# Second layer's softmax divisors moved to GpSimd ahead of the transposes, its output projection in three single-pass parts, a full-height halo product, and reordered units, in a fused two-layer kernel

## The chip, the cores and the metric

One core of a Trainium2 chip. TensorE (PE) multiplies and transposes, ScalarE (ACT) and VectorE (DVE) read its results out of PSUM, GpSimd (POOL) works on SBUF only, SyncE (SP) starts transfers. The metric is the time of one execution on the device in microseconds (us), lower is better, as the median of the runs.

## The reference, cut to what matters

Eight images of 384 rows (256 image rows, 128 text rows) and 256 columns go through an edge filter and a text embedding, then two transformer layers, the second with a mixture of eight experts:

```
edge = abs(conv3x3(gray, scharr)).sum / 2          # rows 0..255 of h
h = h + attn0(LN(h))        # 16 heads of 16, causal; then gelu MLP 256-1024-256 inside
h = h + ternary_ffn(LN(h))  # relu, 256-1024-256
# second layer's attention, on LN(h):
att = q @ k.T / 8 + slope * rel            # 16 heads of 64, 4 key/value heads, causal
m = max(att);  e = exp(att - m)
att = e / (1 + sum(e))                     # the divisor is one number per row and head
out = (att @ v).transpose(...) @ Wo        # Wo is 1024 x 256
h = h + out
h = h + moe(LN(h))          # router, top 2 of 8 experts, capacity 960
```

## The kernel before

The attention runs as 16 units, one for each image and layer. `unit` exists once for each engine, and each holds a hand-written list of short calls; a unit's list is the order of that engine's queue. A call that doesn't apply to a kind of unit (`Kind`) does nothing. Units 0 to 7 are the first layer (`U_FIRST`, five `U_MID0`, `U_SIX`, `U_SEVEN`), unit 8 (`U_EIGHT`) is the second layer's first, then come six `U_MID1` and `U_LAST`. Other work lies between a unit's heads: a first-layer unit carries the convolution of a coming image, the previous image's first projection, MLP and ternary feed-forward (s2); a second-layer unit carries the next image's queries and keys (s1p) and the previous image's projection, norm and router (s3). Units 9 to 14 hold s1p and s3 alone, unit 8 holds s2 and s1p, unit 15 s3 alone. After the units come an epilogue for the last image, the routing, and the experts.

Within a unit the 16 heads go in pairs. `scores(p)` (L962) makes a pair's products into PSUM banks 0 to 2; `mask_max(n)` (DVE, L2286) adds the bias, writes `probs[:, n % 4]` and the row maxima; `exps(n)` (ACT, L1725) exponentiates in place and leaves the row sums in `rowsum`; `turn(n, half)` (PE, L978) transposes a head's six 128 x 128 blocks into banks 3 and 4; `take_turned(n)` copies bank 3 (ACT, L1733) and bank 4 (DVE, L2429) to `probsT[:, n % 4]`; `mix(c)` (PE, L1013) multiplies a pair by the values into bank 5. There are four buffers of `probs` and of `probsT`, and `mask_max(n)` comes behind `take_turned(n - 4)` in DVE's queue. `exps` takes the six instructions of a head: three activations and three reads of the accumulator.

The divisors of the second layer go a way of their own. `invert(c)` (DVE, L2300 to L2302) adds 1 to a pair's sums and takes reciprocals; `spread(c)` (POOL, L3178) copies them into `rinv`, 128 x 384; `divisors(c)` (PE, L989) transposes that in three steps into bank 6 or 7; `take_divisors(c)` (ACT, L1644) copies it to `rinvT`; `weigh(c)` (DVE, L2308) multiplies bank 5 by `rinvT` into `o1T[:, c, :]` and frees bank 5. `spread`, `divisors` and `take_divisors` of the last pair are done in the next unit (`..._last`). The first layer does the same in two groups of eight heads.

`second_rows(t)` (PE, `token_major`, L1030 with tiles `wo,o1T`) is the second layer's projection: for each of three row tiles eight products 128x128 by 128x256 in fp32. The epilogue has its own copy, `rows_out` (L1501). `wo1` is loaded by SP behind unit 8's transfers. An fp32 product is two matmul records in the trace; one whose operands are marked fp32r is one record. Elsewhere the kernel writes an fp32 product as three fp32r products of an upper and a lower part (hi x hi, hi x lo, lo x hi), as in `values` and `second_queries`.

`edges(hf)` (PE, `convolve`) makes half an image: twice six records of L934 with 128 rows, then two of L935, whose operands `halo_gray` and `edge_w` have 3 rows (the neighbouring row of the other half).

Queues: each engine takes its list strictly in order and waits on counters. PE, ACT and DVE share banks 6 and 7 for all dense products, given out by turns (`dense_units`).

Of the kernel before, what the change touches and what calls it, by code (L numbers as in the profile page):

```python
# [20 lines left out]
F32 = mybir.dt.float32  # L21
# [6 lines left out]
P = 128  # L28
# [106 lines left out]
def dense_units(k):  # L135
# [6 lines left out]
    if k.layer == 0:  # L142
        add(k.tail is not None, "rinvT_tail")
        add(True, "v0_0", "v0_1")
        add(k.s2, "proj0_0")
        add(True, "v0_2")
        add(k.s2, "proj0_1")
        add(k.s1, "lnA0", "lnA1")
        add(k.s2, "proj0_2")
        add(k.s1p, "lnB0", "lnB1", "q1_0", "k1_0")  # L150
        add(k.s1, "qk_0", "qk_1")
        add(k.conv, "conv0")
        add(k.s1p, "q1_2", "q1_3")
        add(k.s1, "qk_2")
# [4 lines left out]
        add(k.s1p, "k1_1")  # L159
        add(k.s1, "stk0_0_k", "stk0_1_q")  # L160
        add(k.s2, "down0_0")
        add(True, "rinvT0")
        add(k.s1, "stk0_1_k", "stk0_2_q", "stk0_2_k")
        add(k.s1p, "q1_5", "q1_1")
        add(k.s2, "down0_1", "down0_2")
        add(k.s1p, "q1_6", "q1_4", "q1_7")
# [4 lines left out]
        add(k.s2, "up1_1", "up1_2", "up1_3", "up1_4", "up1_5", "up1_6", "up1_7", "down1_0")  # L171
        add(k.s1, "stk1_1_q", "stk1_1_k")
        add(k.s2, "down1_1", "down1_2")
        add(k.s1, "stk1_2_q", "stk1_2_k")
    else:
        add(k.tail is not None, "rinvT_tail")
        add(True, "v1_0", "rinvT0")
        add(k.s2, "proj0_0")
        add(k.s3, "proj1_0")
        add(k.s2, "proj0_1", "proj0_2")  # L180
        add(k.s3, "proj1_1")
        add(True, "v1_1")
        add(k.s2, "lnM0", "lnM1")
        add(True, "v1_2")
        add(k.s3, "proj1_2")
        add(k.s2, "up0_0", "up0_1")
        add(True, "rinvT1")
        add(k.s1p, "lnB0", "lnB1")
        add(k.s2, "up0_2", "up0_3", "up0_4")
        add(True, "rinvT2")  # L190
        add(k.s1p, "q1_3", "q1_0")
        add(k.s3, "lnE0", "lnE1")
        add(k.s2, "up0_5", "up0_6", "up0_7")
        add(True, "rinvT3")
        add(k.s2, "down0_0")
        add(k.s1p, "k1_0", "q1_5")
        add(True, "rinvT4")
        add(k.s2, "down0_1")
        add(k.s1p, "q1_1")
        add(k.s2, "down0_2")  # L200
        add(k.s1p, "k1_1")
        add(True, "rinvT5")
        add(k.s1p, "q1_2")
        add(k.s2, "lnF0", "lnF1", "up1_0")
        add(k.s1p, "q1_4")
        add(k.s2, "up1_1", "up1_2")
        add(k.s1p, "q1_6")
        add(k.s2, "up1_3", "up1_4")
        add(k.s3, "logits")
        add(k.s2, "up1_5", "up1_6", "up1_7", "down1_0", "down1_1", "down1_2")  # L210
        add(True, "rinvT6")
        add(k.s1p, "q1_7")
    return u


def psum_plan():


# [98 lines left out]
def moved(u, d):  # L317
    return u[0], u[1] + d
# [3066 lines left out]
```

## Time and profile before

| | us |
|---|---|
| median of 3 runs (1877.96 to 1881.28) | 1880.91 |
| the profiled execution | 1881.84 |
| its span, first to last instruction | 1880.0 |
| TensorE busy | 1751.2 (93%) |
| VectorE busy | 1248.4 (66%) |
| ScalarE busy | 967.2 (51%) |
| GpSimd busy | 545.7 (29%) |

```profile
PE   5788999999999999899999999993999999999997
PEld 3455677776867677688888888872898999899896
DVE  5678787777778775857767777667744555454542
ACT  1355657575756766656667666640234334333421
POOL 2352433424242410111111111010434434533431
PEclk9698999999999999999999999995999999999998
```

Each digit is a slice of 47 us in tenths busy, and `PEclk` the clock granted to TensorE in tenths of full speed. The first two slices are the setup, slices 3 to 18 the first layer, 19 to 26 the second layer's attention, 27 and 28 the routing, the rest the experts.

### The profile page before, as it was taken

The numbers are of one execution on the slowest core, as the hardware profiler recorded it, in microseconds if no ns is written. First come the engines' busy times: TensorE is split into PE (matmuls) and PEld (weight loads), VectorE is DVE, ScalarE is ACT, GpSimd is POOL, SyncE is SP. The second block draws the span as 40 slices with busy tenths as digits, with TensorE's granted clock in tenths as the row PEclk, the third lists the DMA queues.
The fourth block names the chain that finished last, engine by engine and source line by source line (L and its number), as shares of the span: only waits on it lengthen the run. The fifth ranks groups of instructions, "written<-read, shape, count | busy, mean of one in ns | idle before, by whom it ended". The sixth has DMA issues, their size and how long they took to land.

```text
span 1880.0 us, 33649 instructions
## 1 busy us (share of the span) xinstructions
PE 1751.2 (93%) x11231; PEld 1427.0 (76%) x11231; DVE 1248.4 (66%) x4073; ACT 967.2 (51%) x2669; POOL 545.7 (29%) x763
## 2 busy tenths in 40 slices
PE   5788999999999999899999999993999999999997
PEld 3455677776867677688888888872898999899896
DVE  5678787777778775857767777667744555454542
ACT  1355657575756766656667666640234334333421
POOL 2352433424242410111111111010434434533431
PEclk9698999999999999999999999995999999999998
DMA  6111020101001010103001110012232321122210
GB/s 212 41 37 66 1 63 10 54 10 54 29 18 60 1 35 1 35 5 92 23 13 35 35 35 27 1 45 68 88 102 68 107 91 54 46 81 67 65 41 22
DMA packets 74244, 91.03 MB, mean 48 GB/s; under 512 B 16524, under 2 KB 64311, under 8 KB 74073
## 3 DMA queue, kind: packets, MB, share of 16 engines
q1 hardware_dynamic: 61464, 67.90, 11.1%
q0 software_dynamic: 9472, 16.77, 3.2%
q10 hardware_dynamic: 3136, 4.21, 0.6%
q8 instruction: 91, 1.49, 0.3%
q14 instruction: 81, 0.66, 0.1%
HBM read 71.02 MB, written 25.00 MB: 51 GB/s over the span
## 4 chain that ended last, share of the span: by engine, by line
PE 75%; issue 9%; DVE 7%; POOL 3%; ACT 2%; DVEq 2%; POOLq 1%; DMA 1%; SPq 0%; ACTq 0%
PE bank L1601 17%; PE bank L1030 16%; PE bank L1616 10%; PE bank L978 7%; PE bank L962 6%; PE bank L1013 6%; PE bank L1190 3%; PE bank L934 2%; PE bank L1052 2%; PE bank L989 1%; PE bank L914 1%; PE bank L935 1%; DVE at_least L2909 1%; POOL rstd_b L3136 1%; PE bank L1582 1%
## 5 line engine op out<-in xcount | busy, mean ns | idle before, releaser
L1725 ACT ACTIVATE probs<-probs,nmax 128x128 f32<-128x128 f32 (+2 forms) x768 | 381.5, 501 | 55.7 <-DVE nmax L2286 55.4
L978 PE MATMUL bank<-cst,probs 128*128 128x128 f32 x1536 | 235.1, 278 | 14.5 <-ACT probsT L1733 11.3
L978 PEld LDWEIGHTS bank<-cst,probs 128*128 128x128 f32 x1536 | 179.8, 142 | 48.1 <-issue 20.1
L3178 POOL COPY rinv<-rowsum 128x384 f32<-128x384 f32 x80 | 40.9, 511 | 563.6 <-DVE rowsum L2302 321.4
L1601 PE MATMUL bank<-xeT,gate_w 128*128 128x480 f32 x768 | 187.5, 379 | 0.5 <-issue 0.5
L1601 PE MATMUL bank<-xeT,up_w 128*128 128x480 f32 x768 | 186.8, 378 | 0.0
L3072 DVE TENSOR_TENSOR prod<-bank,sil 128x480 f32<-128x480 f32 x128 | 84.0, 657 | 147.6 <-PE bank L1601 146.8
L1616 PE MATMUL bank<-down_w,hT 128*120 128x256 f32 x1536 | 181.3, 280 | 0.0
L1616 PEld LDWEIGHTS bank<-down_w,hT 128*120 128x120 f32 x1536 | 179.9, 181 | 0.1
L1733 ACT COPY probsT<-bank 128x384 f32<-128x384 f32 x256 | 121.6, 475 | 107.4 <-PE bank L978 71.9
L1646 ACT ACTIVATE sil<-bank 128x480 f32<-128x480 f32 x128 | 73.0, 570 | 175.8 <-PE bank L1601 175.7
L2429 DVE COPY probsT<-bank 128x384 f32<-128x384 f32 x256 | 141.5, 553 | 30.3 <-PE bank L978 28.6
L1601 PEld LDWEIGHTS bank<-xeT,up_w 128*128 128x128 f32 x768 | 144.8, 189 | 21.6 <-DVE up_w L3004 0.2
L1601 PEld LDWEIGHTS bank<-xeT,gate_w 128*128 128x128 f32 x768 | 144.2, 189 | 21.5 <-issue 0.6
L1725 ACT ACTIVATION_READ_ACCUMULATOR probs<-probs,nmax 128x1 f32 x768 | 146.6, 191 | 0.0
L2286 DVE CUSTOM_DVE_ANT_0 probs<-bank,alibi 128x128 f32<-128x128 f32 (+2 forms) x384 | 141.7, 420 | 2.0 <-issue 0.3
L3354 POOL DMA_INDIRECT out<-ye,slot_token x64 | 75.5, 1180 | 229.7 <-DVE ye L3085 217.8
L2286 DVE CUSTOM_DVE_ANT_0 probs<-bank,cst 128x128 f32<-128x128 f32 (+2 forms) x384 | 140.9, 419 | 0.0
L962 PE MATMUL bank<-k1T,q1T 64*128 64x256 f32 (+2 forms) x768 | 100.5, 394 | 2.9 <-DVE nmax L2286 2.9
L3324 POOL DMA_INDIRECT xe<-xn_rows,slot_token x64 | 70.9, 1108 | 93.0 <-DVEq L3010 52.4
L962 PEld LDWEIGHTS bank<-k1T,q1T 64*128 64x128 f32 x768 | 83.3, 186 | 18.4 <-issue 12.9
L1013 PE MATMUL bank<-probsT,v 128*64 128x384 f32 (+2 forms) x768 | 97.0, 388 | 0.0
(350 smaller groups left out, 3422.3 us busy)
## 6 DMA issues: line engine op xcount, KB each, us to landing
gate_raw<-in_L_ffn_gate_w SPq DMA_DIRECT2D x8, 1024.0 KB, 4.8
up_raw<-in_L_ffn_up_w SPq DMA_DIRECT2D x8, 1024.0 KB, 6.9
down_raw<-in_L_ffn_down_w SPq DMA_DIRECT2D x8, 1024.0 KB, 5.7
img<-in_x SPq DMA_DIRECT2D x8, 768.0 KB, 5.1
residual_rows<-x SPq DMA_DIRECT2D x8, 384.0 KB, 2.5
residual_rows<-h_in SPq DMA_DIRECT2D x8, 384.0 KB, 3.6
xr<-residual_rows SPq DMA_DIRECT2D x8, 384.0 KB, 4.7
hr<-residual_rows SPq DMA_DIRECT2D x8, 384.0 KB, 3.6
```

The lines of the kernel that those rows point to most:

```text
L962: last = mm(scores_place(s, t), q[:, P * t:P * (t + 1)], k[:, 0:P * (t + 1)], start=True, stop=True)
L978: last = tr(ps[bank][:, P * q:P * (q + 1)], probs[:, n % 4, SEG[t] + P * j:SEG[t] + P * (j + 1)], ident)
L1013: last = mm(ps[5][rows_o, P * j:S], w, probsT[:, n % 4, cols_j], start=first, stop=final)
L1030: last = mm(ps[bank][:, 0:width], x, w, start=(k == 0), stop=(k == len(pieces) - 1))
L1601: last = mm(ps[bank][:, 0:HALF], w[:, wp, c, P * m:P * (m + 1)], xeT[:, xp, c, HALF * hf:HALF * (hf + 1)], start=(c == 0 and k == 0), stop ...
L1616: last = mm(ps[bank][:, D * (j % 2):D * (j % 2) + D][0:CP], hT[:, j // 4, hp, m, CP * (j % 4):CP * (j % 4 + 1)], down_w[:, wp, m, :], star ...
L1725: last = f(p, p, ACT.Exp, bias=nmax[:, n % 4, t:t + 1], scale=-1.0, accum_out=rowsum[:, where, t:t + 1])
L1733: nc.scalar.copy(probsT[:, n % 4, 0:3 * P], ps[3][:, 0:3 * P]).then_inc(freed[3], 1)
L2286: last = v.tensor_tensor_reduce(out=probs[:, n % 4, seg(t)], in0=scores_place(n, t), in1=bias[:, P * (2 - t):S], scale=1.0, scalar=BIG, op ...
L2429: v.tensor_copy(probsT[:, n % 4, 3 * P:6 * P], ps[4][:, 0:3 * P]).then_inc(freed[4], 1)
L3072: tt(prod[:, q % 2, :], k[:, 0:HALF], sil[:, q % 2, :], ALU.mult).then_inc(f_, 1)
L3354: g.indirect_dma_start(out_rows, slots(e, j), ye[0:CP, j, :], None, bounds_check=T - 1, oob_is_err=False).then_inc(scattered, 16)
```

## The change

Second layer: `spread`, `divisors` and `take_divisors` are gone. POOL's `scale(n)` multiplies a head's three blocks of `probs` in place by the reciprocals, behind `sums_ready`, and PE's `turn(n, 0)` waits for that instead of for the exponentials. Bank 5 then holds finished outputs: ACT copies them as an upper part (`take_out`), DVE subtracts it for the lower part (`weigh` is now `lower_out`) and frees the bank. `second_rows` and `rows_out` run on the parts, 24 fp32r products a tile. `wo1` is loaded in the middle of unit 8, over `w1`, and split by one cast on ACT and one subtraction on DVE, each 128 x 2048, near unit 8's end. The last pair's divisors are now inverted in its own unit (`invert(7)`).

First layer: `halo_gray` and `edge_w` get 128 partitions, of which 125 are zero, cleared once in the setup; the L935 product runs over all of them. Divisors stay as they were.

All six lists of the units (PE, ACT and DVE for both layers) are in a new order, POOL's in a few places, and the order of banks 6 and 7 with them.

```diff
             def probs_transposed(n, u, half):
-                if half == 0:
+                if half == 0 and u[1] < B:
                     pe.wait_ge(exp_done, at(u, HEADS, n + 1))
+                elif half == 0:
+                    pe.wait_ge(probs_scaled, at(moved(u, -B), HEADS, n + 1))
...
+            def out_pieces(c, t):
+                cols_t = slice(P * t, P * (t + 1))
+                return [(x[:, cols_t], w[:, c, :]) for x, w in (
+                    (o1_hi[:, c], wo1_hi), (o1_hi[:, c], wo1_lo), (o1_lo[c], wo1_hi))]
...
                 def second_rows(t):
                     if k.s3:
                         if t == 0:
-                            pe.wait_ge(wo1_loaded, 64)
+                            pe.wait_ge(wo1_split, 1)
                             pe.wait_ge(freed[5], at(img_a, PAIRS, take0[5] + 2 * B + PAIRS))
-                        token_major(sec, i, "proj1", t, o1T, wo1, 8)
+                        product(sec, i, f"proj1_{t}", [piece for c in range(PAIRS) for piece in out_pieces(c, t)], D)
...
+            def upper_out(u, c):
+                act.wait_ge(probs_used, used_index(1, u, c + 1))
+                nc.scalar.copy(o1_hi[:, c, :], ps[5][:, 0:S]).then_inc(out_upper, 1)
...
+            def lower_out(u, c):
+                dve.wait_ge(out_upper, at(moved(u, -B), PAIRS, c + 1))
+                tt(o1_lo[c][:], ps[5][:, 0:S], o1_hi[:, c, :].bitcast(F32), ALU.subtract).then_inc(freed[5], 1)
...
+                def scale(n):
+                    pool.wait_ge(sums_ready, out_index(1, u, n // 2, 1))
+                    for t in range(NT):
+                        p = probs[:, n % 4, seg(t)]
+                        last = g.tensor_scalar(p, p, rowsum[:, n, t:t + 1], 1.0, ALU.mult, ALU.mult)
+                    last.then_inc(probs_scaled, 1)
...
-            ("img", [P, 3, 2, IMG], F32), ("gray", [P, 2, IMG + 2], F32), ("halo_gray", [3, 2, IMG], F32))
+            ("img", [P, 3, 2, IMG], F32), ("gray", [P, 2, IMG + 2], F32), ("halo_gray", [P, 2, IMG], F32))
-        edge_w = sb("edge_w", [3, 2, 2, P])
+        edge_w = sb("edge_w", [P, 2, 2, P])
```

The start of the second layer's lists before (`-`) and after (`+`), PE first, then DVE, for the units without s2:

```diff
-                    turn(0, 0)
                     scores(1)
                     mix_last()
-                    divisors_last()
                     values(0)
-                    turn(0, 1)
-                    turn(1, 0)
-                    scores(2)
-                    divisors(0)
-                    turn(1, 1)
-                    second_rows(0)
+                    values(1)
+                    turn(0, 0)
+                    turn(0, 1)
+                    second_rows(0)
+                    turn(1, 0)
+                    turn(1, 1)
+                    scores(2)
...
-                    invert_last()
-                    mask_max(2)
-                    mask_max(3)
-                    invert(0)
-                    weigh_last()
-                    take_values(0)
-                    take_turned(0)
-                    mask_max(4)
+                    invert(0)
+                    mask_max(2)
+                    take_values(0)
+                    weigh_last()
+                    mask_max(3)
+                    take_turned(0)
+                    take_values(1)
+                    invert(1)
```

## Rows read from the trace of the kernel before

**Rows 1.** Windows: stretch, length, busy us (instructions) of PE, PEld, DVE, ACT, POOL, clock, DMA

```profile
257.70:343.80 86.10, 84.04 (x544) 63.03 (x540) 67.22 (x226) 54.98 (x163) 31.07 (x51) 1.00 0.11 35
755.80:846.70 90.90, 84.13 (x555) 65.60 (x554) 62.85 (x227) 57.89 (x159) 14.97 (x28) 1.00 0.07 23
904.80:962.90 58.10, 58.10 (x426) 47.20 (x424) 43.06 (x185) 38.17 (x131) 8.40 (x20) 1.00 0.09 29
1195.30:1246.70 51.40, 50.80 (x376) 40.07 (x375) 35.22 (x156) 32.90 (x115) 6.20 (x14) 1.00 0.07 24
```

**Rows 2.** Waits of PE (total us, times, longest): window 257.7:343.8, then 755.8:846.7

```profile
PE bank L1030 <- ACT relu L1646: 0.9, 1, 0.9
PE bank L914 <- DVE xh_b L2208: 0.7, 1, 0.7
...
PE bank L962 <- DVE nmax L2286: 2.9, 2, 1.9
```

**Rows 3.** Chain that ended last, window 904.8:925 (start us, us, what)

```profile
906.79 1.46 PE bank L1013 x12
908.25 0.48 PE bank L989 x3
...
909.09 0.65 PE bank L978 x6
909.74 1.49 PE bank L962 x10
...
912.05 3.46 PE bank L1030 x16
```

**Rows 4.** The same chain, window 336:341: the ternary feed-forward's fp32r products, 256 columns

```profile
336.69 3.83 PE bank L1190 x32
```

**Rows 5.** Timeline of PE, window 271.3:276, one half of a convolution

```profile
271.49 1.46 PE L934 MATMUL bank<-gray,band 128*128 128x256 f32 x6
272.88 0.69 PE L935 MATMUL bank<-halo_gray,edge_w 3*128 3x256 f32 x2
273.50 1.56 PE L934 MATMUL bank<-gray,band 128*128 128x256 f32 x6
...
275.62 0.56 PE L962 MATMUL bank<-k0T,q0T 64*128 64x256 f32 x4
```

**Rows 6.** Groups by form, ACT then DVE: count | busy us, mean ns | idle before

```profile
L1644 ACT COPY rinvT<-bank 128x384 f32<-128x384 f32 x80 | 38.0, 475 | 48.2 <-PE bank L989 48.2
L1799 ACT CAST xs_hi<-bank 128x384 fp32r<-128x384 f32 x16 | 6.9, 481 | 5.9 <-PE bank L914 5.8
L2009 ACT CAST down_w<-down_raw 128x2048 fp32r<-128x2048 f32 x8 | 15.3, 1915 | 122.1 <-PE bank L1616 122.1
...
L2576 DVE TENSOR_TENSOR xs_lo<-bank,xs_hi 128x384 fp32r<-128x384 f32 x16 | 8.1, 546 | 0.0
L3051 DVE TENSOR_TENSOR down_w<-down_raw,down_w 128x2048 fp32r<-128x2048 f32 x8 | 18.3, 2292 | 8.7 <-ACT down_w L2009 8.6
```

**Rows 7.** Groups by form on POOL: a copy, then operations of two tensors by width

```profile
L3178 POOL COPY rinv<-rowsum 128x384 f32<-128x384 f32 x80 | 40.9, 511 | 563.6 <-DVE rowsum L2302 321.4 <-DVE o1T L2308 237.6 <-DVE o0T L2308 4.6
L3161 POOL TENSOR_TENSOR rot<-qk,cst 128x128 f32<-128x128 f32 x84 | 39.0, 494 | 13.6 <-DVE qk L2312 11.3 <-issue 2.2
L3166 POOL TENSOR_TENSOR qk<-qk,cst 128x256 f32<-128x256 f32 x42 | 34.5, 843 | 3.0
L3169 POOL TENSOR_TENSOR qk<-qk,rot 128x512 f32<-128x512 f32 x21 | 26.7, 1269 | 3.3 <-issue 0.4
```

**Rows 8.** Groups by form on DVE: one operation on SBUF, in the first layer, then the second

```profile
L2208 DVE TENSOR_SCALAR x<-h_in,mv_a,rstd_a 128x256 f32<-128x256 f32 x24 | 16.3, 680 | 9.7 <-POOL rstd_a L3136 9.7
...
L2208 DVE TENSOR_SCALAR xh_a<-h_in,mv_a,rstd_a 128x256 f32<-128x256 f32 x24 | 9.7, 405 | 0.0
```

**Rows 9.** The page's costliest groups: a head's exponentials (three activations, busy us, mean ns)

```profile
L1725 ACT ACTIVATE probs<-probs,nmax 128x128 f32<-128x128 f32 (+2 forms) x768 | 381.5, 501 | 55.7 <-DVE nmax L2286 55.4
```

**Rows 10.** Timeline of DVE, window 1240:1275: the last pair's weighting in the epilogue

```profile
1257.32 0.56 DVE L2308 TENSOR_TENSOR o1T<-bank,rinvT 128x384 f32<-128x384 f32 x1 [1.67 <-ACT rinvT L1644]
```

More of the change, by code:

```diff
@@ L231, in psum_plan @@
         units.append([(name, bank_of[name], 1) for name in dense_units(kind)])
-    end = ["rinvT_tail"] + [f"proj1_{t}" for t in range(NT)] + ["lnE0", "lnE1", "logits"]
+    end = [f"proj1_{t}" for t in range(NT)] + ["lnE0", "lnE1", "logits"]
     end = [(name, 6 + k % 2, 1) for k, name in enumerate(end) if not name.startswith("proj1")]
@@ L1278, in unit @@
                     mlp_up(7)
[L1279 removed]
+                    second_queries(5)
                     stack(0, 0, "k")
@@ L1500, in rows_out @@
                     for c in chunks:
-                        last = mm(ps[bank][:, 0:D], o1T[:, c, P * t:P * (t + 1)], wo1[:, c, :],
-                                  start=(c == 0), stop=(c == PAIRS - 1))
+                        for q, (x, w) in enumerate(out_pieces(c, t)):
+                            last = mm(ps[bank][:, 0:D], x, w, start=(c == 0 and q == 0),
+                                      stop=(c == PAIRS - 1 and q == 2))
                     if PAIRS - 1 in chunks:
@@ L2757, in unit @@
-                    mask_max(11)
-                    mlp_rows(0)
-                    take_turned(9)
-                    weigh(3)
-                    mask_max(12)
-                    invert(4)
-                    invert(5)
+                    mask_max(11)
+                    moe_norm(1)
+                    moe_norm(2)
+                    weigh(3)
+                    take_turned(9)
+                    invert(5)
+                    mask_max(12)
+                    mask_max(13)
+                    mlp_rows(0)
@@ L2764, in unit @@
+                    take_moe()
+                    take_queries(5)
+                    invert(6)
                     take_turned(10)
-                    take_queries(5)
-                    mask_max(13)
                     ffn_norm(0)
+                    weigh(4)
+                    take_turned(11)
+                    take_queries(1)
+                    mask_max(14)
                     mlp_rows(1)
-                    take_queries(1)
-                    weigh(4)
+                    take_turned(12)
@@ L2771, in unit @@
+                    mask_max(15)
                     mlp_rows(2)
-                    take_turned(11)
-                    invert(6)
-                    mask_max(14)
                     ffn_norm(1)
                     ffn_norm(2)
-                    take_turned(12)
+                    weigh(5)
+                    take_turned(13)
                     ffn_lower(0)
                     ffn_lower(1)
-                    mask_max(15)
-                    weigh(5)
+                    invert(7)
```

577 lines of the change are left out of this document (306 added, 271 removed).

## The prediction

> **What bounds the kernel now.** I read the page first: TensorE is busy 1751 of 1880 us and no other engine passes two thirds. Such a mean hides stages, so I cut the span into units, by the first transpose of each unit's probabilities, and asked for busy times in each [rows 1]. A second-layer unit (904.8 to 962.9, one of six alike to 0.1 us) shows PE busy for all of its 58.10 us, DVE for 43.06, ACT for 38.17, POOL for 8.40. The view of waits for that window has no line for PE. A first-layer unit takes 86.10 us, of which PE misses 2.06, the largest part one wait of 0.9 for ACT [rows 1, 2]. Unit 8 misses 6.8 us, 2.9 of it on row maxima, and unit 15 misses 0.6 [rows 1, 2]. So from unit 1 to unit 15 the time is the sum of what PE is given, and DVE, ACT and POOL have 15, 20 and 50 us of slack in a second-layer unit. The setup, the routing and the experts are touched at their edges only.
>
> The duration of one record isn't what it costs a full PE, since matmuls overlap; starts have to be subtracted. In the chain six transposes take 0.65 us, so one costs 0.109; sixteen records of the projection take 3.46, so one costs 0.216; 32 fp32r records of 256 columns take 3.83, so one costs 0.120 [rows 3, 4].
>
> **The change part by part.**
>
> *The divisors' transposes.* Each second-layer unit loses eight groups of three. One group costs 3 x 0.109 = 0.33 us (the chain's 0.48 for L989 holds the switch behind a product of another shape, which stays for whatever comes next) [rows 3]. Of 64 groups 63 lie in units: 63 x 0.33 = 20.6 us, all on the path while PE is full.
>
> *The projection.* A tile is 16 x 0.216 = 3.46 us now and 24 x 0.120 = 2.87 us then, 0.59 less [rows 3, 4]. Seven units with three tiles: 21 x 0.59 = 12.4 us. The bound on the other side would be 24 records at more than 0.144, where nothing is left; no fp32r row of this width is near that.
>
> *The halo product.* Between rows, 12 + 4 records of a half image run from 271.49 to 275.62, 4.13 us; sixteen at 0.216 would be 3.46 [rows 3, 5]. The 0.67 us more lies around L935: 272.88 to 273.50 is 0.62 for two records where 0.43 would do, and the record ahead of L935 starts late as well as the one behind. Three rows instead of 128 cost extra at the entry, within and at the exit. With equal shapes this goes, up to zero if it came from something else in these operands. Two halves: 1.34 us a unit, five full `U_MID0`: 6.7 us. Unit 0 is not full on PE, and I count nothing there.
> The Trainium skill (TensorE: Matmul & The Clock Gate, "Why this matters for your kernels") says that a single product with 32 rows takes the same time as one with 128. By that the padding returns nothing; the trace speaks against it, not for the product alone but for its neighbours.
>
> *ACT and DVE.* `rinvT`'s copy (475 ns) gives way to the copy of the upper part (a cast of this form: 481), `weigh` (0.56 us) [rows 10] to `lower_out` (a subtraction of this form: 546 ns): nothing to count [rows 6]. The sums are as before. What is new is the order: bank 5 is now free after product, ACT, then DVE in series, 1.0 us behind the product. The next `mix` is at least 3 us of PE work away, which hides it.
>
> *Scaling on POOL.* 48 new instructions a unit, a head's being 128, 256 and 384 wide; the eight spreads of 0.51 go. The trace has no such operation. Below: one tensor is read, as in the copy of 384 in 0.51 us, which at the same rate and a start of 0.1 is 0.24 + 0.37 + 0.51 = 1.1 us a head. Above: two tensors, 0.49 + 0.84 + about 1.06 = 2.4 us a head [rows 7]. I take 1.3, near the copy, since only one tensor is streamed. A unit's POOL work becomes 8.4 - 4.1 + 16 x 1.3 = 25 us (43 at the upper end), under the 54 us that the unit will take.
> The Trainium skill (GPSIMD Engine Reference, "Engine selection") advises against elementwise work on GpSimd, about 2x slower with two inputs but roughly line-rate with one, and says it shares SBUF interfaces with VectorE; its rate decides nothing here.
> The sharing shows in the rows: DVE's 128x256 normalisation from SBUF takes 680 ns in the first layer, where POOL is busy 31 of 86 us, and 405 ns in the second [rows 1, 8]. Six of these a unit may grow: 6 x 0.28 = 1.7 us of DVE's 15 us of slack.
>
> *The new chain.* `turn(n)` waited for its own head's exponentials. Now a pair's two heads, an inversion and a scaling come first: from the start of `exps(0)`, 2 x 1.49 [rows 9] + 0.4 + 1.3 = 4.7 us, against 1.5. At the start of a unit ACT first has `take_turned(15)` of the unit before (0.5), so `turn(0, 0)` is ready about 5.2 us after `turn(15, 0)`. PE has `turn(15, 1)`, `second_queries(7)`, the router, `scores(1)`, `mix_last` and two `values` for that time: 0.33 + 0.54 + 1.24 + 1.49 + 1.46 + 0.7 = 5.8 us (the two largest in [rows 3], the others from the same view). That hides it by half a microsecond; at 2.4 us a head it is late by 0.5. DVE waits in `invert(0)` with `mask_max(2)` behind it, and ACT waits for that with `exps(2)`; `turn(2, 0)` is then ready about 10.8 us after `turn(15, 0)` and PE comes to it at 11.4, with a projection tile and a pair of scores in between (at 2.4 us: 11.9, late by 0.5). Four buffers hold two pairs. A pair's turn through them is 1.1 (maxima) + 3.0 + 0.4 + 2 x 1.3 + 0.65 + 0.55 = 8.3 us (10.5), and two pairs have 13.4 us in a unit of 53.7. Unit 15 has little else: a pair is 1.46 + 1.49 + 1.31 = 4.3 us of PE, two pairs 8.5. There I expect small waits, 1 to 3 us in the unit, 5 at 2.4 us a head. I take 2.
>
> *Weights in unit 8.* One ACT cast (1.9) and one DVE subtraction (2.3) [rows 6] near the end. PE has two tiles of `ffn_down` there (3.83 us) [rows 4] and the next unit's scores. Nothing if they cover it, 2 us if not. On SP the four loads now stand ahead of `store_rows`, which waits for later work anyway.
>
> *Epilogue.* The projection of the last image is 48 records, 10.4 us, then 72, 8.6. The last weighting started at 1257.32 after 1.67 us of waiting for `rinvT` [rows 10]; DVE's routing work ended just before that wait and now bounds it. Together 1.5 us.
>
> *Order.* The lists can return at most what PE misses: 2.06 x 5 in the full first-layer units, 3.8, 4.4 and 6.8 in units 6 to 8 (two of these from the same view, not among the rows), 25 us in all. They can also add as much. Most moves have no wait of the rows behind them, and for those I count 0, with -10 and +10 us as ends.
>
> *Sum.* 20.6 + 12.4 + 6.7 + 1.5 - 2 = 39.2, from 1881.84 of the profiled execution: 1842.6. One term more: DVE's `mlp_norm(2)`, for which PE waits 0.7 us in each first-layer unit [rows 2], moves ahead of a block of moments. That is 5 x 0.7, of which I take 3. That gives 1839.6, and the median of the runs is 0.9 below the profiled one: **1839 us**, or 2.2% less.
>
> **The rivals.**
>
> *Waits take half of it.* For: the chain above has only half a microsecond of cover at a unit's start, the deep chain has many hand-overs (each some 0.05 to 0.2 us) that I haven't priced, and a unit of 53.7 us leaves DVE 80% busy. Against: 15 us of slack. Price: 2 us in each of seven units, 5 in the last, 3 lost in the first layer's order: 22 us more, 1861.
>
> *The halo returns nothing,* because the cost lies in the operands and not in the shape: 1839 + 6.7 = 1846.
>
> *The order returns most waits of the first layer:* 10 to 15 us more, 1826.
>
> *Slower: GpSimd becomes the bound.* Place: units 8 to 15, `scale`. It fills the unit from (53.7 - 4.3) / 16 = 3.1 us a head, and the unit is slower than before from (58.1 - 4.3) / 16 = 3.4 us, 1.1 us an instruction. For: its operations of two tensors are already at 2.4 us a head, and DVE, busy 75% of the time, shares SBUF access with it [rows 1, 7, 8]. If it took twice that, 4.8 us, a unit would be 81 us, 23 us more than now, seven units 161, less 8 for halo and epilogue: about 2034 us. Against: the first layer's POOL rows are measured beside a DVE just as busy, and a scale reads one tensor. That the change doesn't do what it says can't be, for the instructions are plain.
>
> **How the numbers follow.** Forecast 0.59 (1828 to 1850), half lost to waits 0.19, halo nothing 0.05, order returns more 0.08, within 0.2% (the two reasons of loss together) 0.02, slower 0.07, mostly GpSimd. Faster by over 0.2%: 0.91; within: 0.02; slower: 0.07; 0.2% is about what a measurement of this kernel can tell from none. The range leaves out the slower case and the ends of the outer two: 1823 to 1862. Both ends hold the unknown costs above but for the slower case.
>
> **What would show it.** Units 9 to 14 at 53.5 to 54.5 us with PE still without a wait would prove the first two terms; a wait of `bank L978` on POOL at a unit's start would be the chain. Sixteen convolution records should take 3.46 us from start to start. POOL's scale: 1.1 to 2.4 us a head. Unit 15: 47 to 50 us. First-layer units: 84 to 85 us. If second-layer units stay near 58 with POOL idle less than a fifth, the slower rival holds. I'd be wrong most easily by the price of `scale` and by waits in units 8 and 15.

## The result

The changed kernel takes 1864.03 us (median of four runs, 1860.99 to 1864.70), against 1881.1 in the same comparison: a ratio of 0.9909, 95% interval 0.9895 to 0.9923, or 0.9% less time. The prediction was 1839 us with 1823 to 1862 as its range. The sign is right; less than half of the gain came.

| | us |
|---|---|
| the profiled execution after | 1864.70 |
| its span | 1862.9 |
| TensorE busy | 1720.3 (92%) |
| VectorE busy | 1255.3 (67%) |
| ScalarE busy | 970.3 (52%) |
| GpSimd busy | 693.1 (37%) |

TensorE has 31 us less to do, but the span is only 17 us shorter. The difference is time in which it stands. Windows of the kernel after, in the columns of [rows 1]: units 2, 8, 12 and 15 (the last with the epilogue, which [rows 1] leaves out).

```profile
254.90:340.60 85.70, 83.07 (x543) 63.92 (x542) 68.33 (x226) 55.30 (x161) 30.60 (x51) 1.00 0.11 35
755.40:848.90 93.50, 84.51 (x535) 64.58 (x534) 67.99 (x230) 60.30 (x164) 35.77 (x69) 0.98 0.10 29
1013.50:1068.20 54.70, 54.68 (x424) 43.98 (x423) 42.75 (x184) 37.96 (x130) 26.34 (x60) 1.00 0.10 30
1177.70:1259.00 81.30, 67.36 (x510) 54.53 (x509) 54.41 (x229) 35.08 (x120) 30.01 (x62) 0.92 0.15 54
```

Unit 12 is full, as before. Unit 15 with its epilogue misses 14 us of PE, unit 8 misses 9, and in both the granted clock is under 1.00. (A stretch without work on an engine is called a stand below.) The waits of PE in the kernel after, in unit 2, then unit 8, then unit 15 (total, times, longest):

```profile
PE bank L1076 <- DVE x_parts L2591: 1.4, 1, 1.4
...
PE bank L1049 <- DVE hr L2387: 2.2, 1, 2.2
PE bank L931 <- DVE xh_b L2244: 1.5, 1, 1.5
PE bank L997 <- POOL probs L3254: 1.5, 1, 1.5
PE bank L1049 <- ACT hidT L1663: 1.2, 1, 1.2
...
PE bank L1032 <- ACT probsT L1754: 2.5, 1, 2.5
PE bank L997 <- ACT probsT L1754: 2.2, 2, 1.8
```

The waits of [rows 2] are gone or small (the row maxima of unit 8 fell from 2.9 to 0.3 us), and others stand in their place.

The profiled spans were cut into units by the first record of `scores(1)` of each, and every unit set against the prediction's own sum. This table is worked out from the starts of those records.

```
us                    before   predicted   after    after - predicted
setup and unit 0      169.5    169.5       168.0    -1.5
units 1 to 5          430.3    420.6       429.9    +9.3
units 6 and 7         156.4    156.4       157.5    +1.1
unit 8                 90.9     88.6        93.4    +4.8
units 9 to 14         348.6    322.2       328.9    +6.7
unit 15 and epilogue   78.8     74.9        81.3    +6.4
routing and experts   605.5    605.5       603.9    -1.6
```

Where the clock stays up, a unit's time nearly always repeats to 0.03 us between kernels that don't differ in it (unit 12 is 54.73 to 54.75 in ten profiles, 55.21 in an eleventh), so it is a much finer measure than the total: the setup lies between 90.9 and 97.0 us and the experts between 572.3 and 576.4 with no change in them. Where a stretch of 3.4 us at the 1.2 GHz level falls into a unit in one profile and not in another, the unit moves by 1 to 2.4 us with nothing changed in it: unit 6 takes 81.0 us with one such stretch in the kernel after and 83.4 with two in `switches`, which changes only the second layer, and unit 15 with its epilogue lies between 80.2 and 81.4 in the profiles that don't touch it. The experiments are judged by units, with the clock beside them.

### The profile page after: what moved, and what is told of

It is laid out like the page before. It is cut to its first block, busy times and chain, and to the rows that moved or that the text cites. A ratio compares the mean times of both kernels' runs of the same rounds, so it can differ in the third digit from the quotient of the medians.

```text
span 1862.9 us, 33716 instructions
## 1 busy us (share of the span) xinstructions
PE 1720.3 (92%) x11231; PEld 1413.5 (76%) x11231; DVE 1255.3 (67%) x4074; ACT 970.3 (52%) x2670; POOL 693.1 (37%) x1084
## 4 chain that ended last, share of the span: by engine, by line
PE 65%; issue 13%; DVE 8%; POOL 5%; POOLq 3%; ACT 2%; DVEq 1%; DMA 1%; SPq 0%; ACTq 0%
PE bank L1618 17%; PE bank L1049 12%; PE bank L1633 10%; PE bank L997 6%; PE bank L979 6%; PE bank L1032 5%; PE bank L1214 3%; PE bank L1076 2%; DVE probs L2322 1%; POOLq L3190 1%; POOL rot L3216 1%; POOL rstd_b L3191 1%; ACT probs L1746 1%; DVE at_least L2963 1%; POOLq L3213 1%
## 5 line engine op out<-in xcount | busy, mean ns | idle before, releaser
L3254 POOL TENSOR_SCALAR probs<-probs,rowsum 128x128 f32<-128x128 f32 (+2 forms) x384 | 179.1, 486 | 194.9 <-DVE rowsum L2338 194.7
L3189 POOL TENSOR_TENSOR rstd_b<-mv_b,eps 128x1 f32<-128x1 f32 x72 | 13.8, 192 | 244.6 <-DVE mv_b L2239 244.6
```

The costliest lines, as they stand in the source:

```text
L3254: last = g.tensor_scalar(p, p, rowsum[:, n, t:t + 1], 1.0, ALU.mult, ALU.mult)
```

## The experiments

Three ideas stood at the start: the terms are right and the new order loses what they give; the chain through GpSimd's scaling loses it; or a term itself is wrong.

**The halo product alone,** in the kernel before.

```diff
-("halo_gray", [3, 2, IMG], F32)      -edge_w = sb("edge_w", [3, 2, 2, P])
+("halo_gray", [P, 2, IMG], F32)      +edge_w = sb("edge_w", [P, 2, 2, P])
```

> The kernel before, with nothing but the full-height halo product. Theory A: 0.65 us per half image, units 1 to 5 from 86.07 to 84.8 us, and up to 2.6 us in the setup, whose 8 products run partly at the lower clock: 1881 to 1872 us. Rival (three rows cost no more than 128): 1881 us, and sixteen convolution records still take 4.13 us from start to start.

Measured: 1874.32 us, ratio 0.9964 (0.9951 to 0.9978). Units 2 to 5 take 85.2 us instead of 86.1, which is theory A but 0.4 short of its 84.8. The convolution and its halo lose 0.58 and 0.59 us a unit, 0.3 comes back as waits behind them.

**The reverse:** 3 rows again, in the changed kernel.

```diff
-mm(o, edge_w[:, hf, k, :], halo_gray[:, 1 - hf, :], ...)
+mm(o, edge_w[0:3, hf, k, :], halo_gray[0:3, 1 - hf, :], ...)
```

> The changed kernel with the halo product's operands cut back to 3 of 128 rows; all the rest is the changed kernel. Theory: the convolution and its halo go from 7.0 back to 8.26 us a unit, units 2 to 5 from 85.7 to 86.9 us, or less by what VectorE's wait at stack(1, 0) takes up (the 1.4 us stand shrinks as everything ahead of it comes later): between 86.0 and 86.9. Rival (the halo form is worth nothing in this order): 85.7.

Measured: 1873.59 us in one run. Unit 3 goes from 85.65 to 87.03, and of these 1.38 us 0.69 lie in the twenty-four records of the convolution and 0.68 in the eight of the halo. The timeline of PE of the kernel after, then of this one, shows it:

```profile
274.29 1.46 PE L951 MATMUL bank<-gray,band 128*128 128x256 f32 x6
275.58 0.59 PE L952 MATMUL bank<-halo_gray,edge_w 128*128 128x256 f32 x2
276.01 1.24 PE L951 MATMUL bank<-gray,band 128*128 128x256 f32 x5
...
366.71 1.46 PE L951 MATMUL bank<-gray,band 128*128 128x256 f32 x6
368.10 0.69 PE L952 MATMUL bank<-halo_gray,edge_w 3*128 3x256 f32 x2
368.73 1.56 PE L951 MATMUL bank<-gray,band 128*128 128x256 f32 x6
```

From the start of the pair to the next record: 0.43 against 0.63; and the record ahead of the pair holds PE 0.1 us longer with 3 rows. The term of the prediction, 1.34, is right. Units 3 and 4, at 87.03 and 87.33, lie just above the expected 86.0 to 86.9. (Units 2 and 5 have 3.4 us at the lower clock as well and take 87.93 and 88.06.)
The Trainium skill (TensorE: Matmul & The Clock Gate, "Why this matters for your kernels") has a single product of 32 rows cost what one of 128 costs. No run here has 32 rows; with 3, and products of full height on both sides, the measurement decides against it.

**The divisors alone:** the kernel before without `divisors`, `take_divisors` and `spread` in the second layer; its output lacks the second layer's divisors.

```diff
 def divisors(c):
-    denominators_transposed(sec, i, f"rinvT{c}", k.layer, u, c)
+    if k.layer == 0:
+        denominators_transposed(sec, i, f"rinvT{c}", k.layer, u, c)
...
-tt((o0T, o1T)[layer][:, c, :], ps[5][:, 0:S], rinvT[:], ALU.mult)
+v.tensor_copy(o1T[:, c, :], ps[5][:, 0:S])
```

> The kernel before, with the second layer's spread, divisors and take_divisors left out and a plain copy where bank 5 was multiplied (so its output lacks the second layer's divisors). All orders stay. If 3 transposes at 0.109 us are the price of a group: 64 groups, 20.9 us, 1881 to 1860 us, units 9 to 14 from 58.09 to 55.5. If waits of other engines take the place of PE's work: 1868 us or more.

Measured: 1865.21 us, ratio 0.9911 (0.9892 to 0.9930). Units 9 to 14 take 55.60 us, 2.49 less, where the prediction has 2.6: the transposes take 2.75 with them, and the neighbours get a few tenths back. Unit 15 gives 2.2. Unit 8 gives only 0.7 of the 2.3 that its seven groups should return: it isn't full, and PE's wait there for row maxima grows from 2.9 to 3.6 us. So the term is right where PE is full and 1.6 us too large in unit 8, in the old order already. In all, 1865 lies between the two expected cases.

**The projection alone:** in the changed kernel, the upper parts only, in fp32; its output lacks the lower parts.

```diff
-return [(x[:, cols_t], w[:, c, :]) for x, w in (
-    (o1_hi[:, c], wo1_hi), (o1_hi[:, c], wo1_lo), (o1_lo[c], wo1_hi))]
+return [(o1_hi[:, c, cols_t].bitcast(F32), wo1_hi[:, c, :].bitcast(F32))]
```

> The changed kernel with its projection of the second layer as one full-precision product of each pair's upper part, 8 products of 128 rows and 256 columns a tile, in place of 24 products of parts; the lower parts are still made, but the product leaves them out, so its output lacks them. It measures the term of the projection by itself. Theory: a tile goes from 2.92 back to about 3.4 us, units 9 to 14 from 54.75 to 56.2 to 56.5 us. Rival (the parts cost what they save, by the switches around them): under 55.3 us.

Measured: 1878.55 us in one run; units 9 to 14 go from 54.75 to 56.64, 1.9 us up, somewhat over the expectation, since the transposes around it take 0.2 us longer too. In the chain, the kernel after has a tile in 2.87 us, this one in 3.46:

```profile
1024.15 2.87 PE bank L1049 x24
...
1029.12 3.46 PE bank L1049 x16
```

Those are the two numbers of the prediction to the hundredth.

**The scaling:** the changed kernel without the work and the waits of `scale`; its output lacks the second layer's divisors.

```diff
 def scale(n):
-    pool.wait_ge(sums_ready, out_index(1, u, n // 2, 1))
-    for t in range(NT): ...
+    pass
```

> The changed kernel without the scaling on GpSimd: turn(n, 0) waits for the head's own exponentials as before (so its output lacks the second layer's divisors). Theory B (the longer chain through inversion and GpSimd costs PE its waits in units 8 and 15 and small ones elsewhere): unit 15 with the epilogue falls by 6 us, unit 8 by 2, units 9 to 14 by 0.5 each, 1864 to 1853 us. Rival (the order of the lists makes these waits, whatever scales): within 2 us of 1864.

Measured: 1859.72 us, ratio 0.9880 (0.9858 to 0.9901). Units 9 to 14 gain 0.18 us each on average, unit 15 gains 2.1, unit 8 only 0.15, though PE waits 1.5 us there for a scaling: a wait of 2.3 for the row maxima takes its place. So the whole chain costs about 3.3 us by units, more than the rival allowed and far less than theory B's 11, and isn't the main reason. The forms of the kernel after, on POOL, ACT and DVE:

```profile
L3254 POOL TENSOR_SCALAR probs<-probs,rowsum 128x384 f32<-128x384 f32 x128 | 76.4, 597 | 0.0
L3254 POOL TENSOR_SCALAR probs<-probs,rowsum 128x256 f32<-128x256 f32 x128 | 61.8, 483 | 0.0
...
L3254 POOL TENSOR_SCALAR probs<-probs,rowsum 128x128 f32<-128x128 f32 x128 | 48.6, 380 | 194.9 <-DVE rowsum L2338 194.7
...
L2349 DVE TENSOR_TENSOR o_lo<-bank,o_hi 128x384 fp32r<-128x384 f32 x64 | 35.0, 547 | 7.8 <-ACT o_hi L1727 7.8
L1727 ACT CAST o_hi<-bank 128x384 fp32r<-128x384 f32 x64 | 30.3, 473 | 35.0 <-PE bank L1032 35.0
```

Starts overlap: six scalings in a row take 2.74 us, 1.37 a head, where the prediction took 1.3. The durations rise by about 0.11 us for 128 columns, which leaves 0.27 for the start of each, where the prediction's lower bound took 0.1. POOL waits 195 us in all for DVE's reciprocals, so its own speed isn't the bound.

**The first layer's lists as before,** with all the new parts.

```diff
 # PE, ACT, DVE, POOL and the order of banks 6 and 7, layer 0 only: the lists of the kernel before
```

> The changed kernel, with the first layer's lists of all engines and its order of banks as they were before; the halo product stays at full height, the second layer stays changed. Theory A (the halo product returns its 1.3 us a unit, and the new order of the first layer takes back about as much): units 1 to 5 fall from 85.7 to 86.9 us to 84.8, unit 0 and unit 6 by 1.1 to 1.4, in all 8 us, 1864 to 1856 us. Rival (the order is neutral, the halo term was never there): 1864 us, units at 85.7.

Measured: 1859.22 us, ratio 0.9887 (0.9864 to 0.9909). Units 2 to 5 take 85.18 instead of 85.7 to 85.9, unit 1 85.42 instead of 86.88, unit 0 73.46 instead of 74.46, unit 6 79.70 instead of 81.03. The expected 84.8 wasn't reached. Unit 8 goes up, to 95.21, with two low stretches of the clock instead of one. The order does lose in the first layer; but what in it?

**One addition on GpSimd.** The wait of 1.4 us in unit 2 is TensorE's for `ffn_lower`. The timeline of all engines of the kernel after:

```profile
318.17 1.81 POOL L3289 TENSOR_TENSOR xr<-hr,rows 128x768 f32<-128x768 f32 x1 [0.16 <-issue]
...
318.29 1.84 DVE L2244 TENSOR_SCALAR xh_a<-x,mv_a,rstd_a 128x256 f32<-128x256 f32 x1
...
320.05 1.01 DVE L2591 TENSOR_TENSOR x_parts<-bank,x_parts 128x384 fp32r<-128x384 f32 x2
...
320.74 0.63 PE L1076 MATMUL bank<-ident_r,stk_q 128*128 128x128 f32 x4 [1.42 <-DVE x_parts L2591]
```

VectorE's normalisation takes 0.41 us elsewhere. Here it starts beside GpSimd's addition of two operands and ends with it. Two moves take that apart. First GpSimd's:

```diff
-ffn_residual()
 deviation(LN_ATTN0, 2)
+ffn_residual()
```

> The changed kernel with one statement of GpSimd's list moved: ffn_residual() (one 1.81 us addition of two operands) behind deviation(LN_ATTN0, 2) instead of ahead of it, in the first layer's units. In the changed kernel it runs at 318.17 to 319.98 in unit 2, and VectorE's attn_norm(1), 0.41 us elsewhere, takes 1.84 us beside it (318.29 to 320.13); ffn_lower comes behind it, and TensorE stands 1.4 us. Theory A (the addition holds VectorE): attn_norm(1) falls back to 0.4 us, the stand falls to under 0.3 us, units 2 to 5 go from 85.7 to 84.4 to 84.9, and unit 1, which has in addition 3.4 us at the 1.2 GHz level right behind the stand (86.88 against 85.65 of unit 2), falls to the same time as unit 2, since the level fell only because TensorE stood. Rival B (VectorE's order alone makes the wait): units stay within 0.3 us of 85.7 and the wait only changes its name. Rival C (the clock fell for another reason): unit 2 gains and unit 1 keeps its 1.2 us more.

Measured: 1852.11 us in one run. Units 2 to 5 take 84.30 to 84.62, unit 1 84.65, unit 7 75.14 instead of 76.50. That is theory A. Units 1 to 5, where the norm was held, gain 7.5 us. Units 6 and 7 gain 2.3 more, but there no norm was held, and the statement's move changed no wait for the better: the lines of PE's waits in unit 7 are the same before and after it. What differs is the clock. Windows of unit 7, in the kernel after and in this one:

```profile
678.90:755.40 76.50, 73.04 (x485) 56.85 (x484) 51.08 (x198) 51.90 (x155) 11.39 (x22) 0.98 0.07 22
...
668.00:743.10 75.10, 71.67 (x485) 55.74 (x484) 51.02 (x198) 51.74 (x155) 11.38 (x22) 1.00 0.07 22
```

In `halo_short`, where the statement isn't moved, unit 7 has no low stretch either and takes 75.13; so these 2.3 us can't be laid to the move. (The rest of the 12 is a shorter setup, 2.6, and 0.4 in unit 8.) The timeline of DVE and POOL in this kernel:

```profile
313.61 0.38 DVE L2244 TENSOR_SCALAR xh_a<-x,mv_a,rstd_a 128x256 f32<-128x256 f32 x1
313.90 1.01 DVE L2591 TENSOR_TENSOR x_parts<-bank,x_parts 128x384 fp32r<-128x384 f32 x2
...
314.88 1.84 POOL L3289 TENSOR_TENSOR xr<-hr,rows 128x768 f32<-128x768 f32 x1 [0.16 <-issue]
```

The addition now lies beside copies and maxima that read PSUM, and they keep their length. With the collision gone, the new order of the first layer is 0.6 to 0.9 us a unit faster than the old one (84.3 to 84.6 against the 85.2 of `l0_old_order`). Then VectorE's own order:

```diff
-attn_moments(2)
-attn_norm(1)
 ffn_lower(0)
 ffn_lower(1)
 take_turned(11)
+attn_moments(2)
+attn_norm(1)
```

> The changed kernel with VectorE's attn_moments(2) and attn_norm(1) moved behind ffn_lower and take_turned(11) in the first layer's units; GpSimd's list is as it was. Theory A: TensorE's 1.4 us stand ahead of stack(1, 0) goes here too, because what it waits for no longer stands behind the held norm: units 2 to 5 at 84.4 to 84.9 us, unit 1 the same as unit 2. Rival: GpSimd's addition holds ffn_lower itself or the copy of turn 11, and the wait goes on at 0.7 us or more, units 2 to 5 at 85.2 or over.

Measured: 1864.92 us in one run, units 2 to 5 at 85.22 to 85.53. The stand ahead of `stack(1, 0)` goes, as theory A says, but a wait for ACT's `relu` behind it grows from 0.4 to 1.4 us, and 0.4 us a unit is all that is left. The price named for the rival is met, its mechanism isn't: `ffn_lower` ran beside the addition at its usual length. (In this run a long low stretch of the clock in unit 0 reached into unit 1, so that unit 1 can't be compared.)

**Unit 15.**

```diff
# PE
+scores(7)
 second_queries(1)
 turn(11, 0)
# ACT
 exps(12)
+take_turned(10)
 exps(13)
-take_turned(10)
...
# DVE: take_turned(10), invert(6), mask_max(14), weigh(4), take_turned(11), mask_max(15), take_turned(12), ...
```

> The changed kernel with the order of unit 15 alone written anew around its end: TensorE's scores(7) ahead of turn(11), ScalarE's copies of turned heads 10 and 12 ahead of exps(13) and exps(15), VectorE's maxima of heads 14 and 15 ahead of the weighing of pairs 4 and 5. Theory A (the order loses what unit 15 was to gain: TensorE stands 2.2 and 2.5 us for ScalarE's copies queued behind exponentials, with two stretches of 3.4 us at the 1.2 GHz level behind them): unit 15 with the epilogue goes from 81.3 to 75 to 78 us. Rival B (the chain maximum, exponentials, sum, scaling, transposes of the last heads is what ends last, in any order): 80 us or more. The other units stay within 0.3 us.

Measured: 1860.38 us in one run; unit 15 with the epilogue goes from 81.33 to 76.34, and its two low stretches of the clock are gone. Theory A; since several statements moved at once, the run doesn't say which of them did it. In the kernel after, PE and POOL stand like this:

```profile
1217.00 0.52 PE L997 MATMUL bank<-cst,probs 128*128 128x128 f32 x3 [1.84 <-ACT probsT L1754]
...
1219.68 2.35 PE L979 MATMUL bank<-k1T,q1T 64*128 64x256 f32 x12
...
1227.25 1.59 PE L1032 MATMUL bank<-probsT,v 128*64 128x384 f32 x8 [2.49 <-ACT probsT L1754]
...
1217.41 2.74 POOL L3254 TENSOR_SCALAR probs<-probs,rowsum 128x128 f32<-128x128 f32 x6 [2.30 <-DVE rowsum L2338]
1227.35 2.74 POOL L3254 TENSOR_SCALAR probs<-probs,rowsum 128x128 f32<-128x128 f32 x6 [7.20 <-DVE rowsum L2338]
```

`scores(7)` stands behind `turn(12, 0)`, which needs the scaling that starts at 1217.41; so ACT, which has its exponentials to do, waits 3.1 us for row maxima, and POOL stands 7.2 us for the reciprocals ahead of its last scalings. The score group itself takes 2.35 us instead of 1.57, at the lower clock.

**Shape switches in the second layer.**

```diff
-turn(3, 0)
 scores(3)
+turn(3, 0)
...
 scores(6)
-norm_moe()
 mix(4)
+norm_moe()
```

> The changed kernel with two of TensorE's statements moved in the second layer's units: mix(4) ahead of norm_moe(), so that it stands right behind scores(6), and scores(3) ahead of turn(3, 0). In unit 12 of the changed kernel six transposes take 0.63 us when a projection or query product follows them and 0.80 us between two products of 64 rows or 64 columns; ten groups of transposes are followed by such a product, seven in the kernel before. Theory A (each such switch costs about 0.15 us, and this is what the 0.53 us more of the transposes is): two switches fewer, units 9 to 14 go from 54.75 to 54.4 to 54.5 us. Rival B (the difference lies in waits too small to be listed): 54.7 to 54.8, or slower where scores(3) comes ahead of its bank.

Measured: 1874.29 us in one run, units 9 to 14 at 56.05. Worse, and no test of the theory: the moves made two waits that weren't there,

```profile
1057.32 0.41 PE L1049 MATMUL bank<-xs_hi,wq_hi 128*128 128x384 f32 x1 [0.55 <-ACT xTb L1661]
...
1060.64 1.03 PE L997 MATMUL bank<-cst,probs 128*128 128x128 f32 x6 [0.85 <-ACT probsT L1754]
```

and these 1.4 us cover the 0.3 that was looked for. It does show that a unit without a wait can get one from a single moved statement.

**Unit 8,** by three tries. The first moves three things at once.

```diff
# unit 8 only
-norm_mlp()             # PE: now behind turn(4, 1)
-mask_max(6)            # DVE: now ahead of mlp_norm(0)
-deviation(LN_ATTN1, 1) # POOL: now behind scale(4)
```

> The changed kernel with the order of unit 8 alone altered: VectorE's mask_max(6) ahead of mlp_norm(0), TensorE's norm_mlp() behind turn(4, 1), GpSimd's deviation(LN_ATTN1, 1) behind scale(4). In the changed kernel ScalarE has nothing to do from 770.55 to 777.15 in this unit, TensorE stands 1.5, 0.8 and 0.5 us ahead of the transposes of the norm and of turn 4, and 3.4 us at the 1.2 GHz level follow. Theory A (the order is late for the one unit that carries both layers' work): unit 8 goes from 93.4 to 90.5 to 92.3 us. Rival B (VectorE, busy for all but 0.6 us of 755 to 782, bounds this stretch whatever the order): 93 us or more.

Measured: unit 8 at 96.67 us (1866.50 in one run): PE now stands 5.0 us for two scalings, and theory A fails. The second and the third move one statement each.

```diff
+mix(0)                 # PE, unit 8 only
 norm_mlp()
...
 turn(4, 1)
-mix(0)
```

> The changed kernel with one statement of TensorE's list moved in unit 8 alone: mix(0), the product of the first pair of heads with the values (1.51 us, its operands ready since about 767), ahead of norm_mlp(), for which TensorE stands 1.49 and 0.79 us at 772 to 774.6 while VectorE normalises. Theory A (ready work stood behind a wait): unit 8 goes from 93.42 to 91.0 to 92.0 us, about 1.3 for the stand filled and up to 1 more if the stretch of 3.4 us at the 1.2 GHz level behind it goes too. Rival B (VectorE bounds this stretch): the stand comes back ahead of turn(4) or scores(4), 93 us or more.

Measured: unit 8 at 93.46 (1865.57 in one run), no gain. The product wasn't ready, as I had thought: it needs the last tile of the values, which DVE copies between its norms. Timeline of DVE and PE in this kernel:

```profile
774.95 0.41 DVE L2379 COPY v<-bank 128x256 f32<-128x256 f32 x1
...
775.46 0.91 PE L1032 MATMUL bank<-probsT,v 128*64 128x384 f32 x2 [2.65 <-issue]
```

The third:

```diff
+mlp_rows(0)            # DVE
 mask_max(12)
 mask_max(13)
-mlp_rows(0)
```

> The changed kernel with one statement of VectorE's list moved in the second layer's units (it does nothing but in unit 8): mlp_rows(0), which frees the bank of mlp_down(0), ahead of mask_max(12) and mask_max(13) instead of behind them. VectorE has nothing to do from 804.6 to 808.8, mlp_down(0) ends at 807.2, and TensorE's keys stand 2.21 us for the bank until 813.06. Theory A: that stand goes, unit 8 from 93.42 to 91.0 to 91.6 us. Rival B: what ends last there is the exponentials of heads 12 and 13 (810.84 to 814.20), half a microsecond later by the move, so that the stand moves to turn(12): 92.8 us or more.

Measured: unit 8 at 94.83 (1864.46 in one run). The wait of 2.2 us for the bank turns into two others, and the clock's low stretch in this unit doubles to 6.8 us:

```profile
PE bank L1049 <- DVE q1T L2634: 1.2, 1, 1.2
PE bank L997 <- ACT probsT L1754: 0.8, 1, 0.8
```

**The gains together.** First the two that had worked:

> The changed kernel with the two edits that gained by themselves, together: ffn_residual() behind deviation(LN_ATTN0, 2) in the first layer's units, and the order of unit 15 written anew. Theory (the two losses are independent of each other): units 2 to 5 at 84.3 to 84.6 us, unit 1 at 84.65, unit 15 with the epilogue at 76.3, in all 12.1 + 5.0 = 17 us below the changed kernel's 1864, 1845 to 1849. Rival (they share a cause, so that one of the gains goes): 1851 to 1853.

Measured: 1851.44 us (1850.80 to 1854.93, five runs), ratio 0.9855 (0.9834 to 0.9876). By the total this is the rival's 1851 to 1853, not the expected 1845 to 1849. By units it is the theory: both gains are there in full, 14.9 us together (units 1 to 5 at 84.66, 84.31, 84.32, 84.63 and 84.43, 7.5 in all; units 6 and 7 2.4, which is the clock; unit 15 at 76.33, 5.0). The total is some 3 us above what was expected, because the 12.1 of the single run held 2.6 us of a short setup. Then with unit 8's two moves, though neither had gained by itself:

> The changed kernel with ffn_residual() moved in the first layer, the order of unit 15 written anew, and both moves of unit 8. Theory A (the gains add up): units 1 to 7 and 15 as in residual_last, unit 8 at 89 to 90.5, in all about 3 us under residual_last's 1851.4: 1847 to 1850, about 1.6% under the kernel before. Rival B (the two moves of unit 8 share their gain, or neither returns it): 1850 to 1852.

Measured: 1850.68 us (1847.61 to 1852.26, four runs), ratio 0.9839 (0.9825 to 0.9853). This is rival B. Unit 8 is 94.95 where 89 to 90.5 was expected, 1.5 us behind `residual_last`. Unit 6, which the two moves don't touch, is 82.33 instead of 80.03, with a low stretch of the clock at 616.45 that `residual_last` doesn't have; and the experts of its profile are 3.2 us shorter. Both beat the changed kernel by 0.7%, and neither can be called the better one.

## Why the prediction failed, by its own steps

*The divisors' transposes:* 2.6 us a unit predicted, 2.49 measured (no_divisors). Right in a full unit. "All on the path while PE is full" doesn't hold in unit 8, where PE misses 6.8 us and 0.7 came of 2.3.

*The projection:* 1.77 a unit predicted; the projection's records lose 1.6 in unit 12, and going back costs 1.9 (fp32_proj). Right within 0.2.

*The halo product:* 1.34 predicted, 1.26 less in unit 2 and 1.37 back in halo_short. Right, and so is its reason, the operands' height. With the old lists only 0.9 of it reached a unit's time (halo_alone), which the prediction didn't allow for.

*Scaling on POOL:* 1.3 us a head predicted, 1.37 measured. What was wrong is an inference beside it. [Rows 8] has one norm at a mean of 680 ns, and I put that down to sharing in proportion to POOL's load, "six of these a unit may grow" by 0.28. The two forms of the kernel after:

```profile
L2244 DVE TENSOR_SCALAR xh_a<-x,mv_a,rstd_a 128x256 f32<-128x256 f32 x24 | 16.8, 708 | 2.1 <-POOL rstd_a L3191 2.1
...
L2244 DVE TENSOR_SCALAR x<-h_in,mv_a,rstd_a 128x256 f32<-128x256 f32 x24 | 9.6, 398 | 6.2 <-POOL rstd_a L3191 6.2
```

The slow form has become fast (680 to 398) and another slow, with POOL's first-layer work unchanged: five records of 1.84 us among nineteen of 0.41 make the 708. A mean hid single collisions, and which instruction is hit is a matter of order.

*ACT and DVE, the new chain:* "small waits, 1 to 3 us" in unit 15 were given for the scaling, and it costs 2.1 there and 0.18 in a unit of the middle. Right in size.

*Order:* **this is the step that failed.** The prediction counted 0 for it, with -10 and +10 as ends. Units 1 to 7 lost 10.4 us against the prediction, unit 8 4.8 and unit 15 6.4. "Most moves have no wait of the rows behind them, and for those I count 0" looked for old waits that a move would end, and not for new ones that it would make: what will now run beside what. Two edits of the order alone gave back 12.5 us, beyond the +10 that stood as its end. Of it,
- 7.5 us in units 1 to 5 are one collision of GpSimd's addition with VectorE's norm, which no list of the kernel before had (the same norm has a mean of 413 ns there), with 1.2 us of clock behind it in unit 1. Shown by residual_moved. Another 2.3 in units 6 and 7 are low stretches of the clock whose cause stays open.
- 5.0 us in unit 15 are the order around its end, `scores(7)` and ACT's copies behind work that waits, with two low stretches. Shown by last_order as a whole. The remaining 1.4 stay open; the chain's 2 us were in the forecast already.
- Of the 4.8 us in unit 8, 1.6 are the divisors' transposes, which return only 0.7 of 2.3 there. The other 3.2 stay open. The low stretch isn't it: `residual_last` has none in unit 8 and takes 93.44 against 93.42. That it isn't the scaling or the first layer's lists is shown; that its order can be mended by one move isn't. VectorE is busy for 24.1 of the 26.6 us from 755.4 to 782.0 and each move of a statement only gave the wait another name. That VectorE's load bounds this stretch is only argued, and the kernel before has it busy for 23.4 us in the first 26.6 of the same unit, hardly less.
- 1.1 us a unit in units 9 to 14: 0.2 are the scaling's chain, 0.2 the projection's term, 0.1 the divisors'. The rest, some 0.6, may be where transposes and queries stand. In unit 12 the products take what they took, 12.01 for scores and 11.57 for heads, but the transposes of probabilities take 0.53 more and the queries 0.46 more. Six transposes take 0.75 to 0.80 us if scores or heads follow and mostly 0.57 to 0.63 if a dense product does, and by their starts there are nine groups of the first kind instead of seven (not ten, as I had counted for `switches`): 2 x 0.15 = 0.3 us. Two groups with a dense product behind them took 0.79 and 0.84 all the same. So this covers a part at most, and no experiment shows it, since `switches` made waits of its own.

*`mlp_norm(2)`:* the wait of 0.7 in [rows 2] is gone as predicted, and the 3 us taken for it were paid back in the same units by the collision.

Of the rivals, "waits take half of it" (1861) named this course and nearly its size, with chance 0.19; but it put most of the waits into the second layer's chain, and there they are least. Its "3 lost in the first layer's order" were 10.

## What to carry to other kernels

Price what a reordering brings together, and not only what it separates: for each long GpSimd instruction with two SBUF operands, list VectorE's SBUF instructions that may now start beside it. Read the spread of a form's durations before using its mean; 680 ns was a few of 1.7 to 1.9 us among many of 0.4. Count a term in full only where the engine is full: unit 8, which had waits, kept most of what it was to give. And where one engine is full, measure an edit by the unit in which it lies, with the granted clock beside it: 1.4 us of a wait was plain in an 86 us unit and lost in the scatter of 1864, but one low stretch can move a unit by as much with no edit in it.

## What the hardware showed that I hadn't expected

**GpSimd holds VectorE for a whole instruction.** The norm at 318.29 ended at 320.13, 0.15 us behind the addition's end at 319.98, in each of five units (1.83 or 1.84 us each). The split of the hidden rows, two SBUF operands on VectorE, takes 1.98 us at 325.04 beside the next addition (324.77 to 326.60), and 0.56 with none beside it (837.73). Copies and maxima that read PSUM weren't held: three maxima begun at 323.53 to 324.09, within an addition that ran from 322.97 to 324.81, took their usual 0.29, 0.42 and 0.55 us, and a copy begun at 324.57 its 0.55. Scalings hold a norm too, but they are short: the norm at 872.88 began 0.06 us behind a scaling of 0.48, took 0.56 instead of 0.41 us and ended 0.14 behind it; the most that one grew beside scalings is 0.17. The Trainium skill (SBUF — State Buffer, "SBUF: two separate sides") states this as an exclusive lock on a shared port pair that is held for the full instruction, while the other engine blocks, and that it concerns VectorE's operations with two SBUF inputs or in a two-port mode. The trace agrees: what was held ended 0.15 to 0.42 us behind the addition. The norm reads one tensor; in which mode it ran no run here shows.

**A pause on TensorE may cost twice.** Units 1 and 2 of the kernel after have the same lists and the same stand. Behind it the clock fell for 3.4 us in unit 1 and not in unit 2, and unit 1 is 1.2 us longer (86.88 against 85.65). Windows of the kernel after, the 6 us with the stand and the 3 behind them; then of residual_moved at the same place:

```profile
229.00:235.00 6.00, 3.98 (x28) 2.90 (x28) 5.56 (x13) 3.08 (x11) 4.01 (x7) 0.99 0.01 1
235.00:238.00 3.00, 3.00 (x15) 2.41 (x17) 1.80 (x8) 2.30 (x8) 1.59 (x1) 0.50 0.02 5
...
226.50:232.50 6.00, 5.41 (x41) 4.20 (x44) 5.56 (x20) 4.37 (x13) 4.10 (x7) 1.00 0.00 1
232.50:235.50 3.00, 3.00 (x35) 2.23 (x28) 3.00 (x11) 2.72 (x10) 2.88 (x2) 1.00 0.05 16
```

With PE busy 3.98 of 6 us the clock went to 0.50, the 1.2 GHz level, and fifteen instructions filled 3 us; with 5.41 of 6 it stayed at the 2.4 GHz level, and thirty-five did. In unit 2 the 6 us with the same stand, PE busy for 4.08 of them, left it at 1.00, so the same pause doesn't always cost it. The kernel after has such stretches of 3.4 us in units 1, 6, 7 and 8 and two in unit 15; the kernel before has none from 163 us to 1268, in the last wait of the epilogue, and `residual_last` none from 159 to 1237. In `residual_moved` unit 1's went with the wait, but so did those of units 6, 7 and 8, where the waits stayed. Nor do they cost the same: 1.2 us in unit 1, 1.0 and 1.4 in units 6 and 7, nothing to be seen in unit 8. When a pause costs the clock, these runs don't settle.
